# Scan of a Mamba layer: du x B formed by TensorE against diagonal matrices, in place of ScalarE products turned by TensorE

## The reference, cut to what matters

```python
def step(h, inp):                                   # over t = 0..1023
    d_t, u_t, B_t, C_t = inp                        # delta, u: (b, d); B, C: (b, n)
    dA = jnp.exp(d_t[..., None] * A)                # (b, d, n)
    dBu = (d_t * u_t)[..., None] * B_t[:, None, :]  # (b, d, n)
    h = dA * h + dBu
    y = jnp.einsum('bdn,bn->bd', h, C_t)
    return (h, y)
```

## Time and profile before

| | us |
|---|---|
| median of 3 runs | 2889.66 (2880.05 to 2891.95) |
| the profiled execution, its own time | 2885.97 |
| its span, first to last instruction | 2884.1 |
| scans of batch 0 | 135.9 to about 768 |
| scans of batch 1 | 880.4 to about 1515 |
| ScalarE busy in 500 to 760 us | 259.93 of 260 |

### The profile page before, as it was taken

The page is one execution under the profiler, slowest core; times in us unless marked ns, Lnnn a source line. Parts: engine busy times, 40 slices in busy tenths (PEclk is TensorE's granted clock), DMA queues, the critical chain, the costliest instruction groups (busy, mean ns, idle before and its releaser), DMA issues. The chain is left out here.

```text
span 2884.1 us, 38743 instructions
## 1 busy us (share of the span) xinstructions
PE 2360.6 (82%) x12450; PEld 1196.7 (41%) x12451; DVE 1956.8 (68%) x1790; ACT 1802.8 (63%) x2808; POOL 1314.1 (46%) x493
## 2 busy tenths in 40 slices
PE   7588888888877888888888867788778689969799
PEld 2244444444334444444443423223322555536444
DVE  7699999999768999999993465923841312225520
ACT  5799999999568999999993324065036311112331
POOL 2099998999606999899991111000000210020000
PEclk9799999999988999999998788899989799979999
DMA  2410001000124000100000220010001510020000
GB/s 94 112 50 26 29 26 41 26 29 25 46 62 103 30 25 25 41 29 26 25 19 17 61 89 1 1 35 26 1 23 35 225 37 22 22 79 1 9 0 30
DMA packets 61705, 115.65 MB, mean 40 GB/s; under 512 B 13587, under 2 KB 21907, under 8 KB 60576
## 3 DMA queue, kind: packets, MB, share of 16 engines
q1 hardware_dynamic: 52992, 103.20, 11.1%
q0 software_dynamic: 8608, 11.05, 1.3%
HBM read 86.39 MB, written 27.53 MB: 39 GB/s over the span
## 5 line engine op out<-in xcount | busy, mean ns | idle before, releaser
L1129 POOL TENSOR_TENSOR hs<-hs,c_bc 128x2048 f32<-128x2048 f32 x256 | 1166.3, 4556 | 65.8 <-DVE hs L1180 50.4
L1180 DVE TENSOR_TENSOR_SCAN hs<-decays,carry,ps 128x512 f32<-128x512 f32 x512 | 620.9, 1268 | 10.9 <-PE ps L1207 9.4
L1180 DVE TENSOR_TENSOR_SCAN hs<-decays,ps 128x512 f32<-128x512 f32 x512 | 610.8, 1215 | 25.2 <-PE ps L1207 6.8
L1215 PE MATMUL ps<-hs,sel 128*64 128x512 f32 x2048 | 499.9, 609 | 14.1 <-POOL hs L1129 13.8
L1207 PE MATMUL ps<-ident,dbu_even 128*128 128x128 f32 x2048 | 295.1, 283 | 93.7 <-DVE hs L1180 65.9
L1207 PE MATMUL ps<-ident,dbu_odd 128*128 128x128 f32 x2048 | 294.5, 283 | 92.2 <-DVE hs L1180 61.4
L1143 ACT ACTIVATE decays<-delta_far,A 128x512 f32<-128x512 f32 x512 | 357.4, 711 | 12.0 <-DVE hs L1180 11.8
L1143 ACT ACTIVATE decays<-delta_near,A 128x512 f32<-128x512 f32 x512 | 356.0, 706 | 2.0 <-DVE hs L1180 2.0
L1151 ACT ACTIVATE dbu_odd<-du_turned,b_turned 128x512 f32<-128x512 f32 x512 | 356.6, 708 | 0.0
L1151 ACT ACTIVATE dbu_even<-du_turned,b_turned 128x512 f32<-128x512 f32 x496 | 345.3, 708 | 0.0
L1207 PEld LDWEIGHTS ps<-ident,dbu_odd 128*128 128x128 f32 x2048 | 220.8, 142 | 241.9 <-DVE hs L1180 188.2
(11 more groups left out here) (284 smaller groups left out, 2655.5 us busy)
## 6 DMA issues: line engine op xcount, KB each, us to landing
c_bc<-c_rows SPq DMA_DIRECT2D x256, 128.0 KB, 2.8
o_rows<-osb SPq DMA_DIRECT2D x32, 256.0 KB
u_rows<-u SPq DMA_DIRECT2D x4, 1024.0 KB, 4.5
d_rows<-delta SPq DMA_DIRECT2D x4, 1024.0 KB, 4.2
delta_near<-d_rows SPq DMA_DIRECT2D x4, 1024.0 KB, 9.6
hs<-u_rows SPq DMA_DIRECT2D x4, 1024.0 KB, 6.7
delta_far<-d_rows SPq DMA_DIRECT2D x4, 1024.0 KB, 12.5
w_down<-in_expert_proj SPq DMA_DIRECT2D x1, 4096.0 KB, 36.4
```

Source lines behind the costliest of these rows:

```text
L1129: pool.tensor_tensor(x, x, spread(c_bc[:, g, :], 4), ALU.mult).then_inc(weighed.sem, 1)
L1180: dve.tensor_tensor_scan(hs[:, quad % RING, n, :], decays[:, s % RING, :], ps[:, DBU + s % RING, :], carry[:, at(i * GB, g), blk] if q els ...
L1215: mm = pe.matmul(ps[lo:lo + DB, ACC + quad % 2 * 2 + j // 2, :], k.sel2[:, :], hs[:, quad % RING, j, :], start=False, stop=False, skip_gro ...
```

## The change

The scaled slices and their turns go. In their place ScalarE makes 128x128 matrices that hold B of 128 time steps on the diagonal (the identity scaled for each partition), one for each of the 2 states and 4 chunks, in a tile `b_diag` with two sides. TensorE multiplies 64 columns of `du_t` (the stationary operand) with such a matrix (the moving one, 128 columns): the product is du x B, turned. State 0 goes to PSUM rows 0 to 63, state 1 to rows 64 to 127. A unit then has 8 products in place of 4 transposes.

Since the input and the weights are no longer overwritten, the store of `xn_rows` and the loads for batch 1 with their waits go too. In `scan_inputs` the first group's 8 diagonals are made ahead of taking du, and wait for B alone.

```diff
 def scan_inputs(...):
-            def first_products():
-                if b == 0:
-                    act.wait_ge(xn_stored.sem, xn_stored.at(16))
+            def first_diagonals():
+                act.wait_ge(taken.sem, taken.at(take_no["B", 0, 0]))
+                for n in range(PAIR):
+                    for t in range(QT):
+                        act.activation(b_diag[:, 0, n, t, :], k.ident[:], ACT.Copy, scale=b_t[:, t, n:n + 1])\
+                           .then_inc(prefilled.sem, 1)
+            def take_du():
                 for t in range(QT):
                     take("du", 0, t, du_t[:, t, :], ACT.Copy)
-                for t in range(QT):
-                    act.wait_ge(taken.sem, taken.at(take_no["du", 0, t]))
-                    for n in range(PAIR):
-                        act.activation(first_dbu[:, t, :, n, :], du_t[:, t, :].rearrange("p (b d) -> p b d", d=DB),
-                                       ACT.Copy, scale=b_t[:, t, n:n + 1]).then_inc(prefilled.sem, 1)
...
-            if b == 0:
-                both = flat[0].rearrange("p (c n) -> p c n", c=C)
-                sp.dma_start(k.xn_rows, both[:, :, T:2 * T]).then_inc(xn_stored.sem, 16)
 def scan(...):
-    def product(q, i, g, n, t):
+    def diagonal(q, i, g, n, t):
...
-        chunk = q * QT + t
-        return (room[(g + 1) % 2][:, t, :, n, :], du_t[:, chunk, :].rearrange("p (b d) -> p b d", d=DB),
-                b_t[:, chunk, at(i * (GB * PAIR), (g + 1) * PAIR + n)])
+        return b_diag[:, (g + 1) % 2, n, t, :], b_t[:, q * QT + t, at(i * (GB * PAIR), (g + 1) * PAIR + n)]
...
-            if reload:
-                sp.wait_ge(turned.sem, turned.at(1 + CPB * LOOPS * UNITS))
-                for to, source in reload:
-                    sp.dma_start(to, source).then_inc(again.sem, 16)
...
-                            act.activation(dbu[0], dbu[1], ACT.Copy, scale=dbu[2]).then_inc(made.sem, 1)
+                            act.activation(made_of[0], k.ident[:], ACT.Copy, scale=made_of[1]).then_inc(made.sem, 1)
...
                 for t in range(QT):
-                    mm = pe.transpose(ps[:, DBU + s % RING, t * P:(t + 1) * P],
-                                      room[g % 2][:, t, blk, :, :].rearrange("p n d -> p (n d)"), k.ident[:])
+                    for n in range(PAIR):
+                        mm = pe.matmul(ps[n * DB:(n + 1) * DB, DBU + s % RING, t * P:(t + 1) * P],
+                                       du_t[:, q * QT + t, blk * DB:(blk + 1) * DB], b_diag[:, g % 2, n, t, :],
+                                       start=True, stop=True)
                 mm.then_inc(turned.sem, 1)
```

More of the change, by code:

```diff
@@ L685, in mamba @@
     with ExitStack() as ctx:
-        room = [k.sb(n, [P, QT, NB, PAIR, DB], ctx=ctx) for n in ("dbu_even", "dbu_odd")]
-        flat = [r[:, :, :, :, :].rearrange("p a b c d -> p (a b c d)") for r in room]
+        flat = [k.sb(n, [P, QT * DI * PAIR], ctx=ctx)[:, :] for n in ("xn_room", "scan_weights")]
+        b_diag = k.sb("b_diag", [P, 2, PAIR, QT, P], ctx=ctx)
         XN = flat[0].rearrange("p (c n) -> p c n", c=C)
@@ L697, in mamba @@
             with ExitStack() as bctx:
-                mamba_batch(k, b, a, room, flat, w, w_out, vec, A, diag, bctx)
+                mamba_batch(k, b, flat, b_diag, w, w_out, vec, A, diag, bctx)
 def scan_weights(a, flat):
@@ L708, in scan_weights, with mamba_batch @@
     return (w_in, w_x, w_dt), [(w_in, a["w_in"]), (w_x, a["w_x"]), (w_dt, a["w_dt"])]
-def mamba_batch(k, b, a, room, flat, w, w_out, vec, A, diag, ctx):
+def mamba_batch(k, b, flat, b_diag, w, w_out, vec, A, diag, ctx):
     X = k.X
@@ L716, in mamba_batch @@
     near = k.sb("delta_near", [P, NB, W], ctx=ctx)
-    if b == 0:
-        xn = flat[0].rearrange("p (c n) -> p c n", c=C)[:, :, 0:T]
-    else:
-        xn = flat[0][:, 0:C * T].rearrange("p (c n) -> p c n", c=C)
+    xn = flat[0].rearrange("p (c n) -> p c n", c=C)[:, :, b * T:(b + 1) * T]
     with ExitStack() as c2:
[L722 to L726, removed]
+        scan_inputs(k, b, xn, w, vec, A, diag, zs, du_t, b_t, near, b_diag, c2)
     with ExitStack() as c2:
-        scan(k, b, A, room, du_t, b_t, near, diag, zs, reload, c2)
+        scan(k, b, A, du_t, b_t, b_diag, near, diag, zs, c2)
     tiles = []
@@ L735, in mamba_batch, with scan_inputs @@
     project(k, tiles)
-def scan_inputs(k, b, flat, xn, w, vec, A, diag, zs, du_t, b_t, near, first_dbu, ctx):
+def scan_inputs(k, b, xn, w, vec, A, diag, zs, du_t, b_t, near, b_diag, ctx):
     nc, ps = k.nc, k.ps
@@ L754, in scan_inputs @@
     c_stored, u_stored, d_stored, d_near = k.sig("c_stored"), k.sig("u_stored"), k.sig("d_stored"), k.sig("d_near")
-    xn_stored, again = k.sig("xn_stored"), k.sig("inputs_again")
     magnitude, e_ready = k.sig("magnitude"), k.sig("e_ready")
@@ L802, in _ @@
         def _(pe):
-            if b:
-                pe.wait_ge(again.sem, again.at(16 * 4))
             for n, (kind, h, m) in enumerate(order):
@@ L923, in _ @@
             take_z(1)
-            first_products()
+            first_diagonals()
+            take_du()
         @block.vector
@@ L997, in _ @@
             store_delta(1)
-            if b == 0:
-                sp.wait_ge(xn_stored.sem, xn_stored.at(16))
             sp.wait_ge(u_stored.sem, u_stored.at(16 * CPB))
@@ L1018, in scan_inputs @@
     if b == 0:
-        xn_stored.passed(16)
         a_ready.passed(1)
         prepared.passed(CI + 1)
-    else:
-        again.passed(16 * 4)
 def spread_delta(k, sp, b, h, to, here):
@@ L1030, in spread_delta, with scan @@
         sp.dma_start(to[n * DB:(n + 1) * DB, :, :], rows[:, :, h * W:(h + 1) * W]).then_inc(here.sem, 16)
-def scan(k, b, A, room, du_t, b_t, near, diag, zs, reload, ctx):
+def scan(k, b, A, du_t, b_t, b_diag, near, diag, zs, ctx):
     nc, ps = k.nc, k.ps
@@ L1051, in scan @@
     decay, turned, scanned = k.sig("decay"), k.sig("dbu_turned"), k.sig("scanned")
-    made = k.sig("dbu_made")
+    made = k.sig("diagonal_made")
     weighed, summed, carried = k.sig("weighed"), k.sig("states_summed"), k.sig("carried")
     skipped, gated = k.sig("skipped"), k.sig("gated")
-    u_here, far_here, again = k.sig("u_here"), k.sig("far_here"), k.sig("inputs_again")
+    u_here, far_here = k.sig("u_here"), k.sig("far_here")
     ACC, DBU = 0, 4
@@ L1146, in body @@
                         n, t = divmod(place, QT)
-                        dbu = product(q, i, g, n, t)
-                        if dbu:
+                        made_of = diagonal(q, i, g, n, t)
+                        if made_of:
                             if place == 0:
                                 act.wait_ge(turned.sem, count(turned, q, i, UNITS, 1 + g * NB))
-                            act.activation(dbu[0], dbu[1], ACT.Copy, scale=dbu[2]).then_inc(made.sem, 1)
+                            act.activation(made_of[0], k.ident[:], ACT.Copy, scale=made_of[1]).then_inc(made.sem, 1)
             all_bodies(act, body)
@@ L2368, in build @@
         k.u_rows = nc.dram_tensor("u_rows", (B, P, CI, T), F32).ap()
-        k.xn_rows = nc.dram_tensor("xn_rows", (P, C, T), F32).ap()
         k.ident16 = k.sb("ident16", [P, P], BF16)
```

## The result

| | before | after |
|---|---|---|
| median, us | 2887.18 (2880.05 to 2891.95, 4 runs) | 2975.93 (2971.29 to 2979.38, 4 runs) |
| profiled execution, its own time | 2885.97 | 2971.29 |
| span | 2884.1 | 2969.5 |
| batch 0, first to last scan | 632.2 | 674.4 |
| batch 1, first to last scan | 635.1 | 673.8 |

The ratio is 1.0306, 95% interval 1.0287 to 1.0324: slower by 3%, 89 us. The scans took 80.9 of the span's 85.4 us. The rest differs by 4.5 us. Experiments that left those parts alone differed as much from each other: their stretch after the last scan was 1364.6 to 1373.4 us, and the one between the batches' scans 111.7 to 114.1.

The account below looks back on a forecast made before the run. TensorE was to become the bound in place of ScalarE, at 5.25 us a quad against 4.90: 2885.97 + 90 for the scan + 6 for the starts = 2982 us, 2984 as the runs' median; range 2942 to 3085.

Parts of the forecast that it names:

- What bounds the kernel: In the scan before the change, ScalarE sets 4.90 us a quad; VectorE could do 4.68, GpSimd some 4.7.
- ScalarE's part: In the scan, diagonals last about 0.38 us; a group takes 7.1 us of ScalarE in place of 9.8.
- TensorE's part: In the scan, slots of 0.109 us: turns 3.49 plus sums 1.72, 5.21 us a quad, taken as 5.25.
- The seam: TensorE's loss between 128-column transposes and 64-column products, 0.2 to 0.3 us a quad before; counted at 0.04 after.
- No further hold-up: In the scan, TensorE isn't held up beyond its own work; ScalarE's later wait for the turns is hidden.
- Starts: At each batch's scan start, TensorE's low clock, hidden by slack until now, costs +3 us, +6 in all; ends 0 and +14.
- The stall between the halves: The stall between the two halves of a batch's scan stays as it was.
- The rest at nothing: Outside the scan, first products (5.05 to about 2.4 us, moved ahead), the dropped store and four loads change nothing.
- pairs don't overlap: Rival: TensorE's short products don't run side by side, a quad takes 8.70 us, 3859 us in all; 3%.
- The weight load shows: Rival: TensorE's weight loads aren't hidden under the short slots, 7.0 us a quad, 3424 us (or 6.1 and 3193); 5%.
- TensorE stays hidden: Rival: slots of 0.093 us or less keep TensorE under VectorE and GpSimd, 4.7 us a quad, 2835 us; 4%.
- no change: Rival: TensorE's slots of about 0.1 us and no seam leave the quad at 4.9 us, 2886 us; 4%.

Follow-up runs that it names:

- mixed kernel with 8 changes a quad: Kernel before, one of four time chunks by diagonals and products, three by scaled slices and transposes, transposes first in every unit: 2949.82 us, ratio 1.0227.
- grouped mixed kernel: Kernel before, one of four time chunks by diagonals and products; products of two neighbouring units together, 4 shape changes a quad: 2844.89 us, ratio 0.9870.
- the two mixed kernels: Kernel before with one of four time chunks by diagonals and products, in two orders: 4 shape changes a quad (2844.89 us) and 8 (2949.82 us).
- the run with one state: Changed kernel with the products of state 1 left out, 4 of 8 a unit: 2960.85 us, ratio 1.0277.

## Why the prediction was right

The forecast was 2984 us with a range of 2942 to 3085; measured were 2975.93. By its steps:

- *What bounds the kernel.* Right. ScalarE alone set 4.90 us: with ScalarE relieved, the kernel gained 1.4%, and VectorE came next at 4.69 in second halves. In first halves it was GpSimd with its carry copies (4.77), which the prediction, with one bound of 4.7 for both, did not see. It had read GpSimd in a second half alone, where it makes no copies.
- *ScalarE's part.* Diagonals last 0.388 us, 0.38 by the estimate. Loading ScalarE again left the quads at 5.21.
- *TensorE's part.* Right in mechanism and in the slot: 0.109, 3.49 us of turns, 1.72 of sums. The seam was counted at 0.04 a quad and was 0: 256 x 0.04 = 10 us of the miss. The mixed kernel with 8 changes a quad puts its price at 0.15 us for each change between the shapes; before the change a quad had two, which makes 0.3, the upper end of what the prediction took from the earlier trace rows. By the Trainium skill ("TensorEngine Tiling (Array Packing)", Key Properties) changing the tiling mode drains TensorE. The traces agree in that each change cost 0.15 us; that it is a drain they don't show.
- *No further hold-up.* Right: the product line waited 3.6 us in all.
- *Starts.* Mis-sized: counted +6, measured about -1. The first body of a batch took 42.64 us in both batches, 0.96 over a later one. Before, it took 40.12 and 41.63 us, 0.9 and 2.4 over. The prediction held that slack had hidden the whole cost before; the 2.4 say that it had not in batch 1. And the changed kernel had a full clock where the kernel before had a low one: 1.00 from 924 to 940 us, at the start of batch 1, where the kernel before had 0.53. In batch 0, the window of 140 to 150 us before, after, and in the grouped mixed kernel (the clock is third from the end):

```profile
140.00:150.00 10.00, 6.88 (x30) 5.13 (x31) 9.79 (x10) 10.00 (x18) 7.17 (x4) 0.83 1.06 227
```

```profile
140.00:150.00 10.00, 9.72 (x99) 6.08 (x97) 9.25 (x9) 9.81 (x21) 7.13 (x4) 1.00 1.06 224
```

```profile
140.00:150.00 10.00, 8.22 (x50) 4.52 (x50) 9.82 (x9) 10.00 (x18) 8.22 (x4) 1.00 1.05 229
```

  TensorE's busier start after the change doesn't explain the clock by itself: the two mixed kernels were busy alike here, 8.22 and 8.21 us, with 1.00 and 0.63. Why it rose sooner stays open.

- *The stall between the halves.* Counted as unchanged. The two bodies around it took 6.9 and 6.3 us over the steady ones, against 4.2 and 5.6 before: +3.4 in all. The cause was not tried apart.
- *The rest at nothing.* Right, shown for the store and the loads. The 8 first diagonals took 2.45 us, 2.4 by the forecast. Their move was not tried alone, but ScalarE then sat idle for 9.37 us at the barrier, 6.82 before, and the first scan of batch 0 began at 135.8 us, 135.9 before.

So 256 x (5.21 - 4.904) = +78, -1 at the starts, +3 at the halves and 1 elsewhere: 81, which are the scans' 80.9 us.

That the sum came within 11 us of the profiled execution (2982 against 2971.29) is in part luck: it counted 12 us too much for the quads and 7 too much for the starts, and left out 4 in the scans and 4.5 outside them.

The rivals: *pairs don't overlap* fell by the 0.109 slots, two records in each, and the run with one state shows it from the other side, since each record without a partner takes a whole slot. *The weight load shows* fell too; the Trainium skill's rule for it ("TensorE: Matmul & The Clock Gate", The mechanism), that a load overlaps products only in other row groups, is contradicted here by 16384 loads over all 128 rows, 137 ns long, under slots of 109 ns. That section also names a second way, a load into a background weight buffer; whether these loads went that way no run tells. *TensorE stays hidden* needed slots of 0.093 us and *no change* slots of about 0.1.

## What to carry to other kernels

Work taken off the engine that sets the pace is worth only what separates it from the next bound, here 40 of 2887 us, so price the engine that receives the work by its slots for the same period first; two engines at their bound are balanced by moving a share (one chunk of four gave 1.3%), not all of it. An fp32 product of 64 weight columns takes two passes over its moving columns, each a slot (0.109 us for 128 columns), whether or not a product runs in the other half of the PSUM rows: give it a partner with output in the other half, next to it in the order. Keep products of one shape together in TensorE's order: each change between 128-column transposes and 64-column products cost 0.15 us.

## What the runs showed of the hardware that was not expected

TensorE doesn't need partners to be neighbours, and it doesn't start records strictly in their order. With runs of 4 and of 8 products in one half, each run overlapped the next by 3.5 slots of 0.109 us (units of 0.985 and 1.365 us in place of 0.872), as if each half had a stream of its own that may start some 4 records, two products, ahead of the other. The timeline shows a sum at 606.65 us started ahead of three product records that come before it. What sets that distance, instructions or records, the runs don't tell.
